# Spare TensorE products at two entries, and an attention pipeline whose transposes run one unit earlier

## The chip, the cores and the metric
The kernel runs on one core of a Trainium2 chip. The metric is device time in microseconds (us) of one execution, input loads and output stores included. Five engines work side by side, each through its own in-order list of instructions, and meet only at semaphores: TensorE (PE: matrix products and transposes), VectorE (DVE), ScalarE (ACT), GpSimd (POOL) and SyncE (SP: here only DMAs).

## The reference, cut to what matters
An activation of 4 x 1024 rows of 128 numbers passes through eight blocks, each `x = x + block(layernorm(x))`: a recurrent mixer with experts, a nine-path feed-forward, random-feature attention, the feed-forward again, segment attention, a soft decision tree, a linear recurrence, and the tree again. The change touches the entries of the third block and the whole of the fifth.

```python
# random features ("favor"): 16 heads of width 8, 32 features a head
phi(u) = exp(u @ proj - max(u @ proj)) * exp(-0.5 * sum(u * u)) + 1e-6
out = (phi(Q) @ (phi(K).T @ V)) / (phi(Q) @ sum(phi(K))) @ Wo.T + bo
# segments: 16 heads of width 8, segments of 64 rows
out = attn(q, k, v)                       # 64 x 64 in the own segment
for off in (-2, -1, 1, 2):                # every 4th row of four neighbours
    out += 0.25 * attn(q, k[seg + off, ::4], v[seg + off, ::4])   # if it exists
out = out @ Wo + bo
```

## The kernel before
Everything is float32 and stays on chip, with the 128 channels on the partitions and rows of x along the free axis: `k.X` holds the 4096 columns of x, `k.Y` the normalized ones, handled in eight chunks of 512. PSUM has eight banks of 512 columns: `k.bank[0..7]`, with `k.pair[i]` for two of them. A product with a 512-column float32 operand is recorded as two MATMULs.

`layernorm` (its lines L87 to L122) runs just ahead of either block: a product with `k.center` takes the mean out (L87, PE), ACT squares (L94), a product with `k.mean` gives the variance (L105, PE), ACT takes ln and exp (L114, L116), DVE writes `k.Y` (L122) and counts `ln_out`. Its last variance product lies well ahead of its last L122.

**Random features.** `favor` works on 32 half chunks: 16 of the keys, then 16 of the queries. PE's list starts with a wait for three copies of weights by DVE (`fw_copied`, L1564 to L1568), then a wait for the last of `ln_out`, then `project(0)` (L1581) and `norms(0)` (L1586, eight products of 16 columns). Then step s holds `scores(s)` (L1606, 16 products of 32 x 128), for the first half `gather` (L1622), `values` (L1593, even s), and the next `project` (even s) or `norms` (odd s). ACT copies and squares each projection (L1704, L1705), copies the norms (L1711), takes the exponentials (L1721) and copies the values (L1717). DVE's `statistics` takes maxima of the scores (L1775), adds the norms (L1782) and subtracts (L1786); in steps 1, 5, 9, ... a sum over `k.Y` (L1803) follows.

**Segments.** `segments` works on 64 units, n = 0 to 63, each eight heads of two segments; 16 units make a batch row, eight make one chunk of output. `first()` waits for weights and for the last `ln_out`, then issues six projections of batch row 0 (L1913) into banks 0 to 5. DVE moves the four for keys and values (L2144), ACT the two for queries in eight activations (L2005), POOL copies each fourth row next to its neighbours (L2077). `scores(0)` waits for these queries.

A unit goes through the engines in this order. PE `scores(n)` (L1937) waits until DVE is through with the scores of n-2. DVE `maxima(n)` (L2116, L2117), `shift(n)` (L2125, L2126; it writes one of four buffers `pr[n % 4]`, so it waits for the transposes of n-4). ACT `exp(n)` (L2037). POOL `halve(n)` (L2084), DVE `sums(n)` (L2133, L2135), ACT `weight(n)` (the reciprocal, L2041 and L2043), POOL `weigh(n)` (L2089, L2090). PE `turned(n)`: eight transposes (L1947) into `k.pair[2]`; ACT copies them (L2033). PE `weighed(n)`: 32 products (L1959) into bank 6. After eight units ACT's `heads(t)` (L2049) copies bank 6, PE's `output(t)` (L1977) multiplies by Wo, DVE's `add(t)` (L2140) adds to `k.X`. The first `weighed` of the next eight units waits for `heads(t)`, since it starts bank 6 anew.

What order there is, is written out by hand. Step n of PE's loop holds scores(n), turned(n-4), weighed(n-5), then, by tables of n, a projection of the next batch row (`PROJ`, L1919), the transposes of values (`values_at`, L1970) or an output. These three share bank 7 (`other`); `free()` makes each wait until the one before has been read: a projection by ACT (L2015, or L2005 in two halves for queries), values by ACT (L2026), an output by DVE's add. Step n of ACT's loop holds heads, turned(n-4), exp(n), weight(n-1), and the reads of bank 7. Step n of DVE's holds maxima(n), shift(n), the add, sums(n-1). In steps 65 and 66 PE also issues the first four L87 of the next norm (`after.center`).

Of the kernel before, what the change touches and what calls it, by code (L numbers as in the profile page):

```python
# [50 lines left out]
def plain(buf, c):  # L51

    return buf[:, c * CH:(c + 1) * CH]
# [161 lines left out]
def layernorm(k, block, norm, feed=None):  # L215

    k.ln_done, k.ln_logged = norm.n0 + NCH + PRIMED["ln_out"], norm.n0 + NCH

    @block.tensor
    def _(pe):  # L220
        for c in range(NCH + 2):
            if c >= 2:
                norm.variance(pe, c - 2)
            if c < NCH:
                norm.center(pe, c)
            if feed is not None:
                feed[0](pe, c)

    @block.scalar
    def _(act):  # L230
        activations(act, k, "natural_log_exp_and_others")
        norm.square(act, 0)
        norm.square(act, 1)
        for c in range(NCH):
            if c + 2 < NCH:
                norm.square(act, c + 2)
            norm.deviation(act, c)
            if feed is not None and len(feed) > 2:
                feed[2](act, c)

    @block.vector
    def _(dve):
        for c in range(NCH):
            norm.scale(dve, c)
            if feed is not None:
                feed[1](dve, c)


def ahead(after):
# [1253 lines left out]
def favor(nc, k, block, normalize, after):  # L1503
# [8 lines left out]
    N = 2 * HALF  # L1512
# [61 lines left out]
    def _(pe):  # L1574
# [91 lines left out]
            nc.tensor.matmul(other[:], wT[:, 3 * P:4 * P], o[c % 2], start=True, stop=True).then_inc(k.fv_out, 1)  # L1666

        pe.wait_ge(k.fw_copied, 3)
        pe.wait_ge(k.ln_out, normed)
        project(0)  # L1670
        norms(0)
# [186 lines left out]
def segments(nc, k, block, after):  # L1858
# [7 lines left out]
    N = B * NSEG  # L1866
# [20 lines left out]
    def own(v, b, c):  # L1887
        return v[b % 2][:, c * (NSEG // 2):(c + 1) * (NSEG // 2), 0:SEG]

    PROJ = {0: 0, 2: 1, 3: 2, 4: 3, 7: 4, 11: 5}  # L1890

    def project_at(n):
        return (n // 16 + 1) * 6 + PROJ[n % 16] if n < N - 16 and n % 16 in PROJ else None

    def values_at(n):
        return n // 4 if n < N and n % 4 == 1 else None

    def output_at(n):
        return (n - 14) // 8 if n >= 14 and n % 8 == 6 else None

    @block.tensor
    def _(pe):
# [5 lines left out]

        def first():
            pe.wait_ge(k.sw_in, 7 * 16)  # L1910
            pe.wait_ge(k.ln_out, normed)
            for i in range(6):
                nc.tensor.matmul(k.bank[i][:], k.sg_w[:, (1, 2, 0)[i // 2], :], k.Y[:, i % 2 * CH:(i % 2 + 1) * CH],  # L1913
                                 start=True, stop=True).then_inc(k.sg_proj, 1)

        def project(p):
            b, i = p // 6, p % 6
# [60 lines left out]
            last.append((k.sg_x, t + 1))  # L1978

        first()  # L1980
        for n in range(N + 7):
            if n < N:
                scores(n)
            if 0 <= n - 4 < N:
                turned(n - 4)
            if 0 <= n - 5 < N:
                weighed(n - 5)
            if project_at(n) is not None:
                project(project_at(n))
            if values_at(n) is not None:  # L1990
                values(values_at(n))
            if output_at(n) is not None:
                output(output_at(n))
            if n in (N + 1, N + 2):
                pe.wait_ge(k.sg_arg, n - 2)
                for c in range(2 * (n - N - 1), 2 * (n - N)):
                    after.center(pe, c)

    @block.scalar
    def _(act):  # L2000
# [51 lines left out]
        for c in range(2):  # L2052
            act.wait_ge(k.sg_proj, 5 + c)
            for part in range(2):
                queries(k.bank[4 + c], 0, c, part)
        for n in range(N + 7):
            if n >= 13 and n % 8 == 5:
                heads((n - 13) // 8)
            if 0 <= n - 4 < N:
                turned(n - 4)  # L2060
            if n < N:
                exp(n)
            if 0 <= n - 1 < N:
# [48 lines left out]
    def _(dve):  # L2112
# [37 lines left out]
        for n in range(N + 1):  # L2150
            if n < N:
                maxima(n)
                shift(n)
            if n >= 15 and n % 8 == 7:
                add((n - 15) // 8)
            if n >= 1:
                sums(n - 1)
        add(TURNS - 1)
# [393 lines left out]
```

## Time and profile before

| | us |
|---|---|
| median of 3 executions | 1256.6 (1256.03 to 1257.96) |
| the profiled execution: its time | 1258.29 |
| its span, first to last instruction | 1256.2 |
| PE busy in the span | 1139.7 (91%) |
| DVE busy | 930.1 (74%) |
| ACT busy | 815.3 (65%) |
| POOL busy | 230.7 (18%) |

All stretches below are us from the start of that span. PEclk is the clock granted to TensorE as a share of its upper level, 2.4 GHz; 0.50 is the lower, 1.2 GHz. The mean over the run is 0.95. PE's busy share includes work that took twice as long for the lower clock, so a busy PE says little until the clock of the stretch is read beside it.

### The profile page before, as it was taken

Reading aid. Unit: us, or ns where it says so; the run is one execution under the profiler, and the core shown is the slowest. Engines: PE = TensorE matmul, PEld = TensorE weight load, DVE = VectorE, ACT = ScalarE, POOL = GpSimd, SP = SyncE. Lnnn points to the kernel's source line nnn. Section 1 sums busy time; section 2 is a strip of 40 time slices with the busy share of each in tenths; the row PEclk is TensorE's granted clock in tenths of the full one; section 3 lists DMA queues with packets and bytes.
Section 4 is the critical chain, followed back from the end, with each engine's and each line's share of the span. In section 5 each row is a group of like instructions: output and inputs, shape, how many; then the busy total and the mean of one; then the engine's idle time right before and its main releaser. Section 6 shows DMA issues by size and latency. Waiting matters only on the chain.

```text
span 1256.2 us, 20246 instructions
## 1 busy us (share of the span) xinstructions
PE 1139.7 (91%) x7444; PEld 639.9 (51%) x7452; DVE 930.1 (74%) x1515; ACT 815.3 (65%) x1300; POOL 230.7 (18%) x330
## 2 busy tenths in 40 slices
PE   7899899999999999799998998798888888898787
PEld 3343344444444344377763453476666676463354
DVE  4967788777777767577775666697888896577766
ACT  6967555556556745645676547486777775868674
POOL 1000000000000011100000012486867675000000
PEclk9999999999999989989999999698899988999899
DMA  6000122122211000000000000000000000000002
GB/s 170 1 0 1 55 59 68 63 59 59 67 59 63 5 1 0 10 2 2 2 1 1 0 1 9 0 2 2 2 2 3 15 2 3 9 1 1 0 1 67
DMA packets 26362, 27.19 MB, mean 22 GB/s; under 512 B 4171, under 2 KB 17308, under 8 KB 26268
## 3 DMA queue, kind: packets, MB, share of 16 engines
q1 hardware_dynamic: 25936, 25.91, 6.9%
q8 instruction: 60, 0.98, 0.3%
q14 instruction: 34, 0.28, 0.1%
q10 hardware_dynamic: 332, 0.01, 0.0%
HBM read 23.30 MB, written 2.62 MB: 21 GB/s over the span
## 4 chain that ended last, share of the span: by engine, by line
PE 63%; DVE 17%; ACT 14%; issue 6%; DMA 0%; SPq 0%; DVEq 0%; ACTq 0%
PE psum L730 8%; PE psum L741 8%; PE psum L733 4%; PE psum L990 3%; PE psum L87 3%; PE psum L1937 3%; PE psum L962 3%; PE psum L1606 3%; PE psum L1947 2%; PE psum L1380 2%; DVE N L2126 2%; ACT ln_std L116 2%; ACT ln_std L114 2%; DVE arena L2117 2%; DVE arena L2116 2%
## 5 line engine op out<-in xcount | busy, mean ns | idle before, releaser
L769 ACT ACTIVATE arena<-psum 128x512 f32<-128x512 f32 x128 | 69.5, 595 | 114.5 <-PE psum L730 114.5
L730 PE MATMUL psum<-arena,weights 128*128 128x512 f32 x256 | 122.3, 601 | 1.7 <-DVE N L128 1.0
L741 PE MATMUL psum<-arena,weights 128*128 128x512 f32 x256 | 120.3, 593 | 0.0
L627 DVE SCALAR_TENSOR_TENSOR arena<-diff,vecs,N 128x512 f32<-128x512 f32 x128 | 95.2, 747 | 0.0
L2037 ACT ACTIVATE N<-N 128x1024 f32<-128x1024 f32 x64 | 67.8, 1059 | 41.7 <-DVE N L2126 41.4
L689 DVE SCALAR_TENSOR_TENSOR arena<-arena,psum 128x512 f32<-128x512 f32 x64 | 44.0, 688 | 62.5 <-PE psum L741 62.5
L1937 PE MATMUL psum<-arena 32*128 32x128 f32 x1024 | 84.6, 310 | 4.8 <-ACT arena L2005 4.8
L1937 PEld LDWEIGHTS psum<-arena 32*128 32x128 f32 x1024 | 71.1, 210 | 33.7 <-issue 18.7
L1947 PE MATMUL psum<-ident,N 128*128 128x128 f32 x512 | 77.2, 299 | 10.2 <-ACT arena L2033 9.9
L2033 ACT ACTIVATE arena<-psum 128x1024 f32<-128x1024 f32 x64 | 65.4, 1022 | 30.6 <-PE psum L1947 30.2
L730 PEld LDWEIGHTS psum<-arena,weights 128*128 128x128 f32 x256 | 48.6, 192 | 62.4 <-issue 58.0
L741 PEld LDWEIGHTS psum<-arena,weights 128*128 128x128 f32 x256 | 48.8, 190 | 61.1 <-issue 61.1
L105 PE MATMUL psum<-ln_sq,mean 128*128 128x512 f32 x144 | 73.2, 601 | 3.1 <-ACT arena L150 1.1
L87 PE MATMUL psum<-X,center 128*128 128x512 f32 x128 | 67.0, 618 | 6.5 <-DVE N L165 3.2
L1947 PEld LDWEIGHTS psum<-ident,N 128*128 128x128 f32 x512 | 61.2, 152 | 20.0 <-issue 15.1
L780 ACT ACTIVATE arena<-arena 128x1024 f32<-128x1024 f32 x64 | 68.3, 1067 | 0.0
L2090 POOL TENSOR_TENSOR N<-N,arena 128x512 f32<-128x512 f32 x64 | 67.8, 1060 | 0.0
L2089 POOL TENSOR_TENSOR N<-N,arena 128x512 f32<-128x512 f32 x64 | 66.8, 1044 | 2.1 <-ACT arena L2043 2.1
L2116 DVE TENSOR_REDUCE arena<-psum 128x8 f32<-128x512 f32 x64 | 43.9, 687 | 31.3 <-PE psum L1937 31.2
L733 PE MATMUL psum<-arena,weights 128*128 128x512 f32 x128 | 65.4, 593 | 0.0
L1775 DVE TENSOR_REDUCE arena<-psum 128x32 f32<-128x1024 f32 x32 | 39.2, 1224 | 32.8 <-PE psum L1606 32.8
L2084 POOL TENSOR_TENSOR mixed<-N 128x256 f32<-128x256 f32 x64 | 46.5, 727 | 74.4 <-ACT N L2037 74.3
(332 smaller groups left out, 2484.5 us busy)
## 6 DMA issues: line engine op xcount, KB each, us to landing
arena<-tw_rows SPq DMA_DIRECT2D x64, 256.0 KB, 3.1
out_dram<-arena SPq DMA_DIRECT2D x8, 256.0 KB, 3.6
arena<-in_L_attn_a_x_dram SPq DMA_DIRECT2D x3, 512.0 KB, 7.2
weights<-in_L_attn_a_eWk_dram SPq DMA_DIRECT2D x1, 1024.0 KB, 5.8
arena<-in_L_attn_a_x_dram SPq DMA_DIRECT2D x2, 256.0 KB, 4.1
weights<-in_L_attn_a_eWr_dram SPq DMA_DIRECT2D x1, 512.0 KB, 9.8
tw_rows<-arena SPq DMA_DIRECT2D x2, 128.0 KB, 2.7
tw_rows<-arena SPq DMA_DIRECT2D x1, 256.0 KB, 3.4
```

Of the source, the lines that this page charges most:

```text
L87: self.nc.tensor.matmul(k.bank[c % W][:], k.center[:], self.src(c), start=True, stop=True).then_inc(k.ln_centered, 1)
L105: self.nc.tensor.matmul(k.bank[W + c % self.vary][:], k.mean[:], k.ln_sq[:, c % W, :], start=True, stop=True).then_inc(k.ln_var, 1)
L627: op = nc.vector.scalar_tensor_tensor(mixed[:, n % 4, a, :], k.diff[:, q % 2, :], k.vec((f"cm_k{e}", f"cm_r{e}")[a]), before, ALU.mult, AL ...
L730: op = nc.tensor.matmul(k.bank[2 * (n % 2) + h][:], k.eWk[:, e, h * P:(h + 1) * P], mixed[:, n % 4, 0, :], start=True, stop=True)
L733: nc.tensor.matmul(k.bank[6][:], k.eWr[:, e, :], mixed[:, n % 4, 1, :], start=True, stop=True).then_inc(k.ex_r, 1)
L741: op = nc.tensor.matmul(k.bank[4 + n % 2][:], k.eWv[:, e, h, :], ks[:, (2 * (n % 2) + h) * CH:(2 * (n % 2) + h + 1) * CH], start=(h == 0), ...
L769: op = nc.scalar.activation(kr[:, h * CH:(h + 1) * CH], k.bank[2 * (n % 2) + h][:], ACT.Relu)
L780: nc.scalar.activation(ks[:, n % 2 * 2 * CH:(n % 2 + 1) * 2 * CH], kr, ACT.Square).then_inc(k.ex_sq, 1)
L1937: op = nc.tensor.matmul(scored[half][:, e * P:(e + 1) * P], k.sg_Q[b % 2][at, seg, 2 * j:2 * j + 2, :].rearrange("p h n -> p (h n)"), k.sg ...
L1947: op = nc.tensor.transpose(turned_to[:, e * P:(e + 1) * P], pr[n % 4][:, e * P:(e + 1) * P], k.ident[:])
L2037: nc.scalar.activation(pr[n % 4], pr[n % 4], ACT.Exp).then_inc(k.sg_exp, 1)
L2116: nc.vector.tensor_reduce(mx[n % 2][:, 0:8], mine, AX.X, ALU.max)
```

## The change
A helper issues products of `k.center` with the first chunk of x; nobody reads their result, no semaphore is counted. It is called with four products ahead of the `ln_out` wait in both blocks, and with five behind the six projections of segments. In the loops of segments, PE and ACT handle turned(n-3) in step n rather than turned(n-4), PE handles weighed(n-4), and the tables for bank 7, for heads and for the add move along. The steps after the last unit are one fewer.

```diff
+def keep_busy(nc, k, bank, products):
+    for _ in range(products):
+        nc.tensor.matmul(bank[:], k.center[:], plain(k.X, 0), start=True, stop=True)
 # favor, PE
         pe.wait_ge(k.fw_copied, 3)
+        keep_busy(nc, k, other, 4)
         pe.wait_ge(k.ln_out, normed)
 # segments, tables
-    PROJ = {0: 0, 2: 1, 3: 2, 4: 3, 7: 4, 11: 5}
+    PROJ = {0: 0, 1: 1, 3: 2, 4: 3, 7: 4, 11: 5}
-        return n // 4 if n < N and n % 4 == 1 else None              # values_at
+        return n // 4 if n < N and n % 4 == 2 else None
-        return (n - 14) // 8 if n >= 14 and n % 8 == 6 else None     # output_at
+        return (n - 13) // 8 if n >= 13 and n % 8 == 5 else None
 # segments, PE: first()
             pe.wait_ge(k.sw_in, 7 * 16)
+            keep_busy(nc, k, other, 4)
             pe.wait_ge(k.ln_out, normed)
             ...                                                      # six projections
+            keep_busy(nc, k, other, 5)
 # segments, PE: the loop
-        for n in range(N + 7):
+        for n in range(N + 6):
-            if 0 <= n - 4 < N: turned(n - 4)
-            if 0 <= n - 5 < N: weighed(n - 5)
+            if 0 <= n - 3 < N: turned(n - 3)
+            if 0 <= n - 4 < N: weighed(n - 4)
 # segments, ACT: the loop
-        for n in range(N + 7):
-            if n >= 13 and n % 8 == 5: heads((n - 13) // 8)
-            if 0 <= n - 4 < N: turned(n - 4)
+        for n in range(N + 6):
+            if n >= 12 and n % 8 == 4: heads((n - 12) // 8)
+            if 0 <= n - 3 < N: turned(n - 3)
 # segments, DVE: the loop
-            if n >= 15 and n % 8 == 7: add((n - 15) // 8)
+            if n >= 14 and n % 8 == 6: add((n - 14) // 8)
```

## Rows read from the trace of the kernel before

**Rows 1.** The page, chain that ended last: share of the span by engine.
```profile
PE 63%; DVE 17%; ACT 14%; issue 6%; DMA 0%; SPq 0%; DVEq 0%; ACTq 0%
```
**Rows 2.** Windows: stretch, length, busy us of each engine (instructions), clock, DMA.
```profile
527.50:546.00 18.50, 17.29 (x86) 13.63 (x86) 9.04 (x10) 5.10 (x9) 0.00 (x0) 0.54 0.00 1
795.50:818.40 22.90, 20.80 (x100) 13.23 (x100) 15.80 (x27) 9.25 (x19) 10.57 (x13) 0.50 0.00 0
```
**Rows 3.** Windows of 1 us, the same columns, where the clock falls.
```profile
528.00:529.00 1.00, 0.63 (x2) 0.00 (x0) 0.00 (x0) 0.33 (x1) 0.00 (x0) 0.95 0.00 0
781.00:782.00 1.00, 0.00 (x0) 0.00 (x0) 0.45 (x2) 0.56 (x1) 0.00 (x0) 0.74 0.00 0
```
**Rows 4.** Timeline, entry of favor: start, us, engine, line, tiles, count, [idle before <-releaser].
```profile
524.83 0.68 DVE L1568 COPY weights<-psum 128x512 f32<-128x512 f32 x1
526.70 0.69 DVE L122 TENSOR_TENSOR Y<-psum,ln_std 128x512 f32<-128x512 f32 x1 [0.55 <-ACT ln_std L116]
527.54 1.10 PE L1581 MATMUL psum<-Y,weights 128*128 128x512 f32 x2 [3.40 <-DVE Y L122]
529.81 1.89 PE L1586 MATMUL psum<-weights,arena 128*128 128x16 f32 x8 [1.18 <-ACT arena L1705]
533.75 1.23 DVE L1775 TENSOR_REDUCE arena<-psum 128x32 f32<-128x1024 f32 x1 [6.36 <-PE psum L1606]
543.29 1.22 DVE L1775 TENSOR_REDUCE arena<-psum 128x32 f32<-128x1024 f32 x1
```
**Rows 5.** Timeline, entry of segments.
```profile
782.43 8.31 PE L1913 MATMUL psum<-Y,weights 128*128 128x512 f32 x12 [3.40 <-DVE Y L122]
789.98 5.46 ACT L2005 ACTIVATE arena<-psum,weights 128x512 f32<-128x512 f32 x8 [8.42 <-PE psum L1913]
795.49 2.08 PE L1937 MATMUL psum<-arena 32*128 32x128 f32 x16 [4.75 <-ACT arena L2005]
797.61 0.69 DVE L2116 TENSOR_REDUCE arena<-psum 128x8 f32<-128x512 f32 x1 [3.42 <-PE psum L1937]
823.37 0.68 DVE L2116 TENSOR_REDUCE arena<-psum 128x8 f32<-128x512 f32 x1
```
**Rows 6.** Timeline, the same kinds of product at the upper clock.
```profile
521.29 1.02 PE L87 MATMUL psum<-X,center 128*128 128x512 f32 x2
548.61 1.06 PE L1586 MATMUL psum<-weights,arena 128*128 128x16 f32 x8
549.60 1.16 PE L1606 MATMUL psum<-weights,arena 32*128 32x128 f32 x16
```
**Rows 7.** Timeline, units of segments: a free pair of maxima, and two waits.
```profile
1039.87 0.68 DVE L2116 TENSOR_REDUCE arena<-psum 128x8 f32<-128x512 f32 x1
1043.30 0.68 DVE L2116 TENSOR_REDUCE arena<-psum 128x8 f32<-128x512 f32 x1
850.75 1.08 PE L1959 MATMUL psum<-arena,ln_sq 128*32 128x64 f32 x32 [2.10 <-ACT arena L2049]
854.93 0.69 DVE L2116 TENSOR_REDUCE arena<-psum 128x8 f32<-128x512 f32 x1 [3.43 <-PE psum L1937]
894.54 1.12 PE L1919 MATMUL psum<-Y,weights 128*128 128x512 f32 x2 [1.77 <-DVE X L2140]
896.80 0.69 DVE L2116 TENSOR_REDUCE arena<-psum 128x8 f32<-128x512 f32 x1 [1.40 <-PE psum L1937]
```
**Rows 8.** Waits, 820 to 1070: who for whom, us in total, times, longest.
```profile
DVE arena L2116 <- PE psum L1937: 23.6, 27, 3.4
```
**Rows 9.** The page, costliest groups: ACT's exp of a unit; busy us, mean ns.
```profile
L2037 ACT ACTIVATE N<-N 128x1024 f32<-128x1024 f32 x64 | 67.8, 1059 | 41.7 <-DVE N L2126 41.4
```
**Rows 10.** Timeline, the last unit of segments.
```profile
1061.46 1.06 POOL L2090 TENSOR_TENSOR N<-N,arena 128x512 f32<-128x512 f32 x1
1066.20 1.04 PE L1947 MATMUL psum<-ident,N 128*128 128x128 f32 x8
1068.35 0.65 PE L1959 MATMUL psum<-arena,ln_std 128*32 128x64 f32 x32 [0.53 <-ACT arena L2033]
```

More of the change, by code:

```diff
@@ L1980, in _ @@
         first()
-        for n in range(N + 7):
+        for n in range(N + 6):
             if n < N:
                 scores(n)
+            if 0 <= n - 3 < N:
+                turned(n - 3)
             if 0 <= n - 4 < N:
-                turned(n - 4)
-            if 0 <= n - 5 < N:
-                weighed(n - 5)
+                weighed(n - 4)
             if project_at(n) is not None:
@@ L2055, in _ @@
                 queries(k.bank[4 + c], 0, c, part)
-        for n in range(N + 7):
[L2057 to L2060, printed above, removed]
+        for n in range(N + 6):
+            if n >= 12 and n % 8 == 4:
+                heads((n - 12) // 8)
+            if 0 <= n - 3 < N:
+                turned(n - 3)
             if n < N:
@@ L2153, in _ @@
                 shift(n)
-            if n >= 15 and n % 8 == 7:
-                add((n - 15) // 8)
+            if n >= 14 and n % 8 == 6:
+                add((n - 14) // 8)
             if n >= 1:
```

## The prediction, made before the change was run
> **What bounds the kernel now.** I read the chain that ended last first: PE holds 63% of it and no other engine a fifth [rows 1], so PE's rate decides wherever the change works. Then the windows with the clock beside the busy time. In favor's first 18.5 us PE is busy 17.29 us at a clock of 0.54; in the first 22.9 us of segments' loop it is busy 20.80 at 0.50 [rows 2]. The one-microsecond windows show what came before each fall: PE stands idle for 3.40 us until the last L122, and the clock is at the lower level (1.2 GHz) from the end of window 528:529 in favor, and inside 781:782 in segments [rows 3, 4, 5]. There it falls twice: the six projections run mostly at half clock (8.31 us for twelve MATMULs), the clock returns, then PE waits 4.75 us for the queries and `scores(0)` takes 2.08 us, against 1.16 for 16 products of that shape at the upper level [rows 5, 6]. Behind the entries, in 820 to 1070, DVE is nearly the bound: free maxima stand 3.43 us apart [rows 7], and it still waits 23.6 us for scores [rows 8]. That sum is what a better order of the units could win at most; a worse order can add to it.
>
> **Favor, four spare products.** One costs two MATMULs, 0.43 us each at the upper clock: the pair's records take 1.02 with their overlap [rows 6], and I use 0.86. Four are 3.44 us. They start when DVE's copy ends, 524.83 + 0.68 = 525.5, and end at about 529.05. The projection starts at 527.54 now [rows 4], so it becomes 1.5 us late: they are longer than the gap they fill. What they may buy is the clock. From the projection to the norms is 2.27 us now (527.54 to 529.81) and stays so, since that projection already ran fast: norms at 531.3. At the upper clock the norms hold PE 1.0 rather than 1.9, `scores(0)` 1.16 rather than 2.08 [rows 4, 6]; DVE's first reduction comes at 533.5, now 533.75. Then values(0) and project(1), a microsecond each, stand ahead of scores(1): it ends at 536.6. Statistics take DVE 2.75 us, to 539.4, the sum over Y 1.2 more, so the third statistic starts at 540.6; now it starts at 543.29 [rows 4]. Gain 2.7 us. Further on the gain is not more, although PE could be earlier: the third projection's copies on ACT stand behind exp(2), which stands behind that third statistic, and norms(2) and scores(4) wait for them. Bounds: +1.5 if the clock falls all the same (every step as now, but late); on the other side PE's 17.29 us at 0.54 would be 9.3 at full clock, 8 less, with the 1.5 paid, -6.5. I take -2.7, from the walk along the rows.
>
> **Segments, the entry.** PE is free from 779.0 (782.43 less 3.40) and the weights are long in. Four products fill 779.0 to 782.45; the projections start at 782.43 now [rows 5], so these cost nothing. That cover is exact: with the clock at the lower level for part of them they would take up to 6.9 us and delay the projections by up to 3.4. At the upper clock six projections take 5.2 us. ACT starts on the queries after the fifth, 782.45 + 5 x 0.86 + 0.1 = 786.9, now 789.98: 3.1 us sooner. Its 5.46 us end at 792.4. The five spare ones behind the projections run 787.6 to 791.9, hidden behind ACT by 0.5 us; without ACT's span they would cost their full 4.3. DVE's moves and POOL's copies of keys start with the projections and stay ahead of the queries. So scores(0) comes 3.1 us sooner, at the upper clock.
>
> From maxima(0) to maxima(6) now pass 25.8 us (797.61 to 823.37) [rows 5]; at 3.43 a unit six take 20.6. So between 0 and 5.2 us more. The full 5.2 needs a clock that holds through new waits: project at n = 1 waits until ACT has read the one before, which lies behind exp(0), some 4.4 us after scores(0) ends (2.6 of DVE, four pieces like the 0.68 of [rows 7]; 1.06 for exp [rows 9]; some 0.7 for the copy), while PE has 2.2 us of work. I take 3: the clock probably falls once in the first few units, as it does now in the loop, and returns. The row of a fall behind a wait of this size is 850.75: 2.10 us idle, and the next 32 products took 1.08 us [rows 7], as long as at half clock.
>
> The Trainium skill speaks against this step ("TensorE: Matmul & The Clock Gate", "A second HAM failure mode: psum-queue depth-cycling"): short idles between groups of matmuls, often enough, make the clock swing between its levels though no one gap is long. This trace agrees at 850.75. By that rule the units gain nothing and only the 3.1 stay; it is rival A below.
>
> **A unit sooner, steady.** Turned(n-3) needs weigh(n-3), two steps of POOL closer. By the order on the engines, scores(n) is held by shift(n-2), and weigh(n-3) ends about 0.5 us after that shift (3.43-us units), when scores(n) still runs for 0.6 us: no wait, margin 0.6 us. DVE's shift no longer waits for transposes; that wait comes only at half clock, where PE is the bound anyway, so I count it nothing. What moves is bank 7 and bank 6. (a) The wait of weighed for heads stays (850.75, idle 2.10; DVE then waits 3.43) [rows 7], but values no longer stand between it and the next scores: 0.6 us less, four times, -2.4. (b) An output at n%8 = 5 is now followed by values at n%8 = 6, whose free() wants the add of DVE's own step n, behind shift(n): 2.6 + 0.74 us after the scores end, while PE has 1.6 us of work. PE idles 1.8 us, as now at 894.54 (1.77), where DVE lost 1.40 [rows 7]. There a projection followed; with values it is about 1.0. Now such a place occurs only before a projection at n = 7 of a batch row, twice; then seven times: 7 x 1.0 - 2 x 1.6 = +3.8. (c) Values leave n = 9, where they waited for ACT's half of the queries: -0.4 three times. (d) At n = 4 the heads wait now precedes a projection: +0.4 three times. Sum +1.4. Bounds: -8 where waits shrink enough that falls of the clock go (a third of the 23.6 of [rows 8]); +14 where each of seven new waits costs what 850.75 does, 3.4, less what is paid now. I take +1.
>
> **The end.** Now turned(63) runs at 1066.20, although POOL was through at 1062.5, because turned comes behind four products of the next norm in each of two steps; weighed(63) is at 1068.35 [rows 10]. A step sooner, turned(63) stands behind only the first batch of these, about 1063.6, and weighed(63) behind the second, about 1066.9: -1.5, and all of the next norm moves with it. Bounds 0 to -3.
>
> **Sum.** -2.7 - 3.1 - 3 + 1 - 1.5 = -9.3. The profiled execution took 1258.29, so 1249.0 for it; it stands 1.7 above the median of 1256.6. On the median: 1247.5.
>
> **Rivals.**
> A. The clock is lost again within a few units. Segments keeps 3.1 and the tail 1.5, favor about half of its gain or pays the 1.5, the loop +1 to +2: 1253 to 1255. For it: waits of 1 to 2.3 us in units 1 to 3, sparse products in favor. Against it: 894.54, where after 1.77 idle the scores still came in time with a loss of only 1.40.
> B. Slower: the add. Values at n%8 = 6 stop PE seven times for 1.8 us, two steps behind the heads wait of the same group; the clock falls at most of them and scores double. At 3.4 each, +24, less the 3 now paid, less 0.6 x 4, and less 10.3 won elsewhere: +8, 1264. It makes the kernel slower from about five of seven at that price (17 - 3 - 2.4 - 10.3 = +1). For it: [rows 7]. Against it: the heads wait alone already costs a fall at most places now, so many of the falls would only move.
> C. Better than forecast: the first units run at full clock (another 2.2), and falls in the loop go, since PE gets its work in evener steps: 5 more. 1240.
> D. The spare products don't hold the clock: 1.5 lost in favor, nothing won at either entry but the loop's shift: 1257.
>
> **Chances.** Forecast 0.45 (its own range 1244 to 1251), A 0.20, B 0.12, C 0.17, D 0.06. A difference under 0.2%, 2.5 us, can't be told from none. Faster: forecast, C and most of A, 0.77. Same: the rest of A and most of D, 0.11. Slower: B, 0.12. Range 1239 to 1257: it takes in C, the forecast and A, and leaves out B and the far ends.
>
> **What would show it.** Right: clock 1.00 in all 1-us windows from 524 to the first scores of favor and from 779 to scores(0) of segments; the first L1586 of favor at 531.3 with 1.06 us; favor's third L1775 at 540.6; the twelve MATMULs of L1913 in 5.2 to 5.3 us; L2005 starting 4.5 us after L1913; L1937 at once 1.16. In the loop a wait PE L1970 <- DVE L2140, seven times near 1.8, while DVE L2125 <- PE L1947 is gone. Wrong: L1913 still at 8 us (D); 0.50 in most windows of the first 15 us of the loop (A); DVE's waits for L1937 in the loop well over 23.6 us, each behind an L1970 (B); PE waiting for POOL L2090 ahead of L1947, for which I left 0.6 us.

## The result and the profile after

The changed kernel took 1242.4 us (median of 4 runs, 1237.8 to 1246.9) against 1257.3 (4 runs): ratio 0.988, interval [0.983, 0.993]. Measured once more in a later session it was 1240.95 (6 runs) against 1257.41 (11 runs), 0.9879 [0.9843, 0.9916]. The forecast was 1247.5 with a range of 1239 to 1257: the sign is right, but the gain is some 15 us and not 9, and most of it does not come from where the forecast put it. 1242.4 lies outside the forecast's own 1244 to 1251, between it and the 1240 of rival C.

Executions of one kernel differ here by up to 14 us. Some 5 us of it lie ahead of everything that was changed (the first 200 us run at a mean clock between 0.97 and 1.00 in kernels with the same code there), so the stages are compared by their own lengths and not by the total alone. A length of a stage comes from one profiled execution of each kernel; where several kernels share the code of a stage, all their lengths are given. The profiled execution took 1246.88 us with a span of 1244.7; the one of before 1258.29 and 1256.2.

The page of after: busy time and share of the span by engine, and the chain that ended last.
```profile
PE 1134.5 (91%) x7470; PEld 629.8 (51%) x7478; DVE 929.9 (75%) x1515; ACT 816.4 (66%) x1300; POOL 231.2 (19%) x330
PE 61%; DVE 18%; ACT 12%; issue 7%; POOL 1%; DMA 0%; SPq 0%; DVEq 0%; ACTq 0%
```
PE holds 61% of the chain where it held 63% [rows 1], DVE one point more.

The timeline of after, entry of favor (start, us, engine, line, tiles, count, [idle before <-releaser]). L252 is the spare product, L1587 the projection, L1592 the norms, L1612 the scores.
```profile
526.28 3.70 PE L252 MATMUL psum<-X,center 128*128 128x512 f32 x8 [1.44 <-DVE weights L1574]
529.82 1.02 PE L1587 MATMUL psum<-Y,weights 128*128 128x512 f32 x2
532.02 1.06 PE L1592 MATMUL psum<-weights,arena 128*128 128x16 f32 x8 [1.17 <-ACT arena L1712]
533.01 2.01 PE L1612 MATMUL psum<-weights,arena 32*128 32x128 f32 x16
549.52 1.32 PE L1592 MATMUL psum<-weights,arena 128*128 128x16 f32 x8 [2.94 <-ACT arena L1712]
550.77 2.08 PE L1612 MATMUL psum<-weights,arena 32*128 32x128 f32 x16
```
Windows of after over the same stretch (the clock is the third figure from the end):
```profile
526.00:533.00 7.00, 5.54 (x18) 2.79 (x18) 1.56 (x3) 2.44 (x5) 0.00 (x0) 1.00 0.00 0
533.00:538.00 5.00, 5.00 (x27) 3.92 (x26) 2.64 (x3) 0.41 (x2) 0.00 (x0) 0.51 0.01 3
550.00:556.00 6.00, 6.00 (x60) 5.25 (x60) 2.64 (x3) 1.53 (x3) 0.00 (x0) 0.52 0.01 3
```
The gap before the projection is filled and the norms run in 1.06 us, as forecast. Then the clock goes to the lower level all the same: at 533 behind an idle of 1.17, at 550 behind one of 2.94, and a third time at 570.7. The second is norms(2) waiting for ACT, a wait that the prediction named as a bound on the gain and did not take for a risk to the clock. Counted from the last L122 (the end of the norm ahead of favor), the third statistic comes 0.2 us later than before, the sixth 3.3 and the tenth 5.0; 1.7 come back at the twentieth, where the kernel before has a fall (604 to 607) and this one has none. To favor's last statistic pass 138.9 us, before 135.5: favor lost 3.3 us.

The timeline of after, entry of segments (L1921 first projections, L2014 queries, L1946 scores, L1928 later projections, L2125 maxima).
```profile
786.49 5.42 PE L1921 MATMUL psum<-Y,weights 128*128 128x512 f32 x12
791.75 4.46 PE L252 MATMUL psum<-X,center 128*128 128x512 f32 x10
796.66 1.16 PE L1946 MATMUL psum<-arena 32*128 32x128 f32 x16 [0.47 <-ACT arena L2014]
797.87 0.69 DVE L2125 TENSOR_REDUCE arena<-psum 128x8 f32<-128x512 f32 x1 [2.51 <-PE psum L1946]
802.20 1.55 PE L1928 MATMUL psum<-Y,weights 128*128 128x512 f32 x2 [2.23 <-ACT arena L2024]
803.68 2.08 PE L1946 MATMUL psum<-arena 32*128 32x128 f32 x16
821.40 0.68 DVE L2125 TENSOR_REDUCE arena<-psum 128x8 f32<-128x512 f32 x1
1040.96 0.69 DVE L2125 TENSOR_REDUCE arena<-psum 128x8 f32<-128x512 f32 x1 [0.93 <-PE psum L1946]
```
Against [rows 5]: the twelve MATMULs take 5.42 us and not 8.31, the scores 1.16 and not 2.08, and from the first projection to maxima(0) pass 11.38 us where 15.18 did. At unit 1 PE waits 2.23 us for the keys, and the clock is down for ten microseconds.

Windows of after, segments' loop.
```profile
775.00:802.00 27.00, 24.43 (x82) 10.60 (x81) 15.49 (x22) 17.01 (x28) 4.77 (x9) 1.00 0.00 1
803.00:813.00 10.00, 9.72 (x49) 6.36 (x48) 7.82 (x14) 6.48 (x14) 6.56 (x8) 0.50 0.01 2
820.00:860.00 40.00, 34.40 (x620) 26.97 (x619) 37.00 (x65) 33.74 (x64) 31.15 (x37) 1.00 0.01 2
900.00:940.00 40.00, 35.73 (x595) 26.46 (x592) 36.39 (x64) 33.49 (x65) 30.92 (x36) 1.00 0.01 2
980.00:1020.00 40.00, 36.39 (x622) 30.09 (x623) 36.51 (x64) 27.98 (x53) 27.55 (x31) 0.87 0.04 12
```
Windows of before, the same stretches.
```profile
820.00:860.00 40.00, 35.20 (x564) 27.22 (x565) 34.23 (x60) 32.40 (x62) 30.30 (x36) 0.87 0.01 2
900.00:940.00 40.00, 35.11 (x559) 27.65 (x557) 33.62 (x60) 30.33 (x60) 27.10 (x31) 0.87 0.01 2
980.00:1020.00 40.00, 34.50 (x571) 28.29 (x570) 35.46 (x62) 29.82 (x58) 27.90 (x31) 0.87 0.04 12
```
In the first 40 us PE does 56 more instructions in less busy time. From maxima(6) to maxima(63) pass 219.56 us, before 230.27: 10.7 us, nearly the whole result, from the part that the forecast gave +1.

Waits of after, 815 to 1045 (who for whom: us in total, times, longest us).
```profile
DVE arena L2125 <- PE psum L1946: 16.2, 29, 1.0
PE psum L1979 <- DVE X L2149: 12.4, 7, 1.8
PE psum L1956 <- POOL N L2099: 8.2, 16, 1.2
PE psum L1968 <- ACT arena L2058: 4.9, 7, 1.1
```
The same of before, 818 to 1055.
```profile
PE psum L1959 <- ACT arena L2049: 9.9, 7, 2.4
PE psum L1947 <- ACT arena L2033: 7.3, 9, 1.7
DVE N L2125 <- PE psum L1947: 5.0, 8, 0.7
```
The wait of the weighing for the heads, 1.95 to 2.39 us at four places and under 1 us at three, is now at most 1.1; seven waits of 1.8 for the add have come. DVE's own waits for scores went from 23.6 [rows 8] to 16.2, and none is over 1.0 us where one was 3.4. DVE's waits for the transposes (the last line), 5.0 us in eight, are gone; all eight stood at the lower clock.

How such a wait and the clock go together in the kernel before: the heads wait of unit 29 (919.69), then the scores, which slow down on their way, and the clock in the windows.
```profile
919.69 0.65 PE L1959 MATMUL psum<-arena,ln_sq 128*32 128x64 f32 x32 [2.39 <-ACT arena L2049]
920.86 1.59 PE L1937 MATMUL psum<-arena 32*128 32x128 f32 x16
920.00:921.00 1.00, 1.00 (x31) 0.74 (x22) 0.59 (x2) 1.00 (x2) 0.14 (x1) 1.00 0.00 0
921.00:922.00 1.00, 1.00 (x14) 1.00 (x16) 0.00 (x0) 0.97 (x5) 0.52 (x1) 0.71 0.00 0
```

The two spans by stage: to the last L122 +0.7; favor +3.3; between favor's last statistic and segments' first projection 0.0; to maxima(0) -3.8; to maxima(6) -2.2; to maxima(63) -10.7; to the last output +0.35; behind it +0.8. Together -11.5, the difference of the spans.

### The profile page after: what moved, and what is told of

Its sections match the earlier page's. It is cut to its first block, busy times and chain, and to the rows that moved or that the text cites. A ratio compares the mean times of both kernels' runs of the same rounds, so it can differ in the third digit from the quotient of the medians.

```text
span 1244.7 us, 20296 instructions
## 1 busy us (share of the span) xinstructions
PE 1134.5 (91%) x7470; PEld 629.8 (51%) x7478; DVE 929.9 (75%) x1515; ACT 816.4 (66%) x1300; POOL 231.2 (19%) x330
## 4 chain that ended last, share of the span: by engine, by line
PE 61%; DVE 18%; ACT 12%; issue 7%; POOL 1%; DMA 0%; SPq 0%; DVEq 0%; ACTq 0%
PE psum L736 8%; PE psum L747 8%; PE psum L739 4%; PE psum L87 4%; PE psum L996 4%; PE psum L968 3%; PE psum L1946 3%; PE psum L1612 2%; PE psum L1386 2%; DVE arena L2126 2%; DVE N L2135 2%; PE psum L105 2%; ACT ln_std L114 1%; ACT ln_std L116 1%; ACT N L2046 1%
## 5 line engine op out<-in xcount | busy, mean ns | idle before, releaser
L1956 PE MATMUL psum<-ident,N 128*128 128x128 f32 x512 | 72.8, 287 | 12.0 <-POOL N L2099 11.0
L1946 PEld LDWEIGHTS psum<-arena 32*128 32x128 f32 x1024 | 64.9, 193 | 26.5 <-issue 13.8
L1946 PE MATMUL psum<-arena 32*128 32x128 f32 x1024 | 77.4, 291 | 0.5 <-ACT arena L2014 0.5
L87 PE MATMUL psum<-X,center 128*128 128x512 f32 x128 | 69.8, 642 | 6.5 <-DVE N L165 3.2
L1956 PEld LDWEIGHTS psum<-ident,N 128*128 128x128 f32 x512 | 57.3, 145 | 21.9 <-POOL N L2099 16.1
L2098 POOL TENSOR_TENSOR N<-N,arena 128x512 f32<-128x512 f32 x64 | 66.9, 1045 | 2.1 <-ACT arena L2052 2.1
L2125 DVE TENSOR_REDUCE arena<-psum 128x8 f32<-128x512 f32 x64 | 43.9, 686 | 22.2 <-PE psum L1946 22.0
L94 ACT ACTIVATE ln_sq<-psum 128x512 f32<-128x512 f32 x72 | 41.9, 591 | 28.0 <-PE psum L87 28.0
```

The costliest lines, as they stand in the source:

```text
L87: self.nc.tensor.matmul(k.bank[c % W][:], k.center[:], self.src(c), start=True, stop=True).then_inc(k.ln_centered, 1)
L1946: op = nc.tensor.matmul(scored[half][:, e * P:(e + 1) * P], k.sg_Q[b % 2][at, seg, 2 * j:2 * j + 2, :].rearrange("p h n -> p (h n)"), k.sg ...
L1956: op = nc.tensor.transpose(turned_to[:, e * P:(e + 1) * P], pr[n % 4][:, e * P:(e + 1) * P], k.ident[:])
```

## Experiments

The first four take the change apart, on one chip beside the kernel before (1256.37, 27 runs). A ratio and its interval are not the quotient of the medians; the two differ by up to 0.2%.

**Favor's four spare products alone.** The kernel before, plus
```
         pe.wait_ge(k.fw_copied, 3)
+        keep_busy(nc, k, other, 4)
         pe.wait_ge(k.ln_out, normed)
```


> The kernel before with the four spare products ahead of the last ln_out wait of favor alone. My theory of the result: they hold the clock through the projection, it falls all the same about 3 us later in some executions, so the gain of 2.7 us that I forecast is there in some and a loss of up to 3 in others: ratio 0.997 to 1.002, and the spread of the executions wider than that of before. Rival 1, the prediction as it stood: -2.7 us, ratio 0.998, clock 1.00 up to the first scores. Rival 2, the spare products only cost their excess over the gap: +1.5, ratio 1.001.

1258.47 us (12 runs), ratio 1.0026 [1.0002, 1.005]: they cost. From the last L122 to the last statistic 138.8 us, as in the changed kernel; the clock fell at 531, 542, 549 and 569. The forecast's -2.7 is out. The excess of 1.5 alone lies inside the interval, but not the stage's 3.3; and the executions do not spread wider than those of before (8.9 us against 12.1), so the expected mixture of gains and losses is not seen.

**The nine at segments' entry alone.** The same line with 4 in `first()` of segments and one with 5 behind its six projections.

> The kernel before with the four and five spare products at the entry of segments alone, the loop as before. Theory 1 (the loop's own order is what took away the falls of the clock): first reduction of scores 3.8 us sooner after the first projection, the six units after it 2 us sooner, and then the same falls of the clock in the loop as before, so -5 to -6 us in all, ratio 0.9955. Rival (the clock in the loop hangs on the entry, the new order adds little): falls go here too, -12 to -16 us, ratio 0.989.

1250.80 (12 runs), 0.9975 to before [0.9952, 0.9998], -5.6 us by the medians (by the interval -6.0 to -0.3). First projection to maxima(0) 11.38 us (-3.8), to maxima(6) 23.64 (-2.1); maxima(6) to (63) 231.7, as before, with the clock at 0.84 to 0.96 in the 40-us windows. So the entry gives what it gives at the entry, and nothing of the loop's gain is its work: the rival is out.

**The loop alone, no spare products.**
```
-    PROJ = {0: 0, 2: 1, 3: 2, 4: 3, 7: 4, 11: 5}
+    PROJ = {0: 0, 1: 1, 3: 2, 4: 3, 7: 4, 11: 5}
-        return n // 4 if n < N and n % 4 == 1 else None
+        return n // 4 if n < N and n % 4 == 2 else None
-                turned(n - 4)
+                turned(n - 3)
```
(with weighed, heads, output and add one step sooner, as in the change)

> The changed loop of segments without any spare product. Theory 1 (the loop's order takes the falls of the clock away by itself): units 6 to 63 take 219 to 221 us as in the changed kernel, entry as before, -9 to -12 us in all, ratio 0.992. Rival (as I forecast for the loop: +1, end -1.5): ratio 1.000, with windows at half clock behind the heads waits as before.

1244.68 (10 runs), 0.9917 [0.9888, 0.9946], -11.7 us by the medians. The profiled execution, 1236.04, is one of its two fastest. Its windows:
```profile
820.00:860.00 40.00, 34.90 (x594) 26.52 (x594) 37.02 (x65) 33.83 (x61) 31.36 (x36) 1.00 0.01 2
900.00:940.00 40.00, 35.49 (x612) 26.38 (x612) 36.57 (x64) 31.58 (x58) 30.72 (x36) 1.00 0.01 2
980.00:1020.00 40.00, 33.35 (x632) 27.27 (x633) 38.65 (x69) 30.48 (x58) 30.36 (x34) 1.00 0.02 5
```
The clock never falls in them, and maxima(6) to (63) takes 217.18 us, 13.1 less than before. Since nothing fills a gap here, the order alone keeps the clock; the rival, the forecast's +1, is out. From maxima(6) to maxima(63) the old loop has seven falls in each of its three profiles (before, favor alone, entry alone), 41 to 44 us at the lower clock. The new one has none here (one comes just behind maxima(63)), 2 in after with 10 us, and 16 in nine profiles together (after, this one, and those of the experiments below but for the two that alter the loop).

Where these falls stand, for every wait of PE of 1 us or more: how many waits there are, and how many had a fall within 4.4 us of the start of the idle.

| PE waits for | us | waits | falls |
|---|---|---|---|
| old order, three profiles: the heads | 1.9 to 2.4 | 12 | 12 |
| the add | 1.8 | 6 | 3 |
| ACT's copy, ahead of transposes | 1.7 | 6 | 3 |
| ACT's queries, ahead of values | 1.2 | 3 | 3 |
| new order, nine profiles: the add | 1.8 | 63 | 17 |
| the heads | 1.1 to 1.3 | 27 | 0 |
| POOL, ahead of transposes | 1.0 to 1.2 | 28 | 1 |

(Two of the 17 come just behind maxima(63).) So four of the old loop's seven falls go with the heads, and the other three with waits that the new order moved as well.

**The change without favor's four.**

> The changed kernel without the four spare products of favor; segments as changed. Sum of theory 1: -16 us against before, ratio 0.987 to 0.988, and a narrower spread than the changed kernel's 1237.8 to 1246.9, since favor's clock is what makes two groups of times. Rival: the two groups come from segments and stay here.

1239.14 (6 runs), 0.988 [0.9846, 0.9914], -17.2 us by the medians: the sum of the two parts (-5.6 - 11.7 = -17.3). By the ratios it is 0.9975 + 0.9917 - 1 = 0.989. The parts add within their intervals, and favor's products are the only one with the wrong sign. Its executions spread over 6.9 us, the changed kernel's over 9.1, and two of its six stand 3 us under the rest; that favor makes two groups of times is not shown.

**Two in favor instead of four** (a second chip, before 1256.88, 8 runs; the next three too).

> The changed kernel with two spare products at favor's entry in place of four: 1.7 us of work for a gap of 1.9 us. Theory (the four cost their 1.5 us excess, and favor's clock falls later for idles inside its first units, whatever the entry does): the projection 0.1 us behind the last L122 again, the clock falls once or twice in the first 30 us, statistics 0 to 31 take 128 to 131 us; 1 to 3 us less than the changed kernel. Rival (the entry decides favor's clock, and two do as well as four): statistics 0 to 31 in 126 us or less and no window under 1.00.

1239.85 (4 runs), 0.9874 [0.9846, 0.9901]. The timeline of its entry:
```profile
525.55 1.98 PE L252 MATMUL psum<-X,center 128*128 128x512 f32 x4 [1.44 <-DVE weights L1574]
527.43 1.12 PE L1587 MATMUL psum<-Y,weights 128*128 128x512 f32 x2
529.73 1.07 PE L1592 MATMUL psum<-weights,arena 128*128 128x16 f32 x8 [1.18 <-ACT arena L1712]
530.72 1.16 PE L1612 MATMUL psum<-weights,arena 32*128 32x128 f32 x16
```
Two end just as the norm does; the projection is not late and the first scores take 1.16. The clock falls later and for shorter (532 to 536 and 539 to 543, before 529 to 546). That is the theory; the rival is out, since maxima of statistics 0 to 31 take 127.3 us. From the last L122 to the last statistic, in all profiles:

| in favor | us |
|---|---|
| none (before and six kernels) | 135.5, 135.5, 135.5, 135.5, 135.1, 133.7, 138.3 |
| two (this and two later ones) | 132.5, 132.5, 132.5 |
| four (after, alone, after again) | 138.9, 138.8, 140.8 |

Against the usual 135.5 two win 3.0 us, four lose 3.3 to 5.3. The table is of the stage; by the total this kernel and the one with none (1239.14) are not told apart. One kernel with none, at 138.3, is nearly as slow as those with four: there a second fall came at 545, where the usual profile has none until 599.

**The later gaps of favor filled.** One more spare product ahead of norms(0), three ahead of norms(2), with four at the entry.
```
         def norms(c):
+            if c in (0, 2):
+                keep_busy(nc, k, k.bank[6], 1 if c == 0 else 3)
```


> The changed kernel, and one spare product into bank 6 ahead of norms(0), three ahead of norms(2), where PE stood idle 1.2 us and 2.9 us. Theory (the clock of favor falls behind these idles, of which I had named the second only as a bound on the gain): clock 1.00 from the entry to at least 560, the fourth to sixth statistics 3.1 to 4.1 us apart in place of 6.0 and 6.0, -4 to -6 us against the changed kernel, so about 0.984 of before. Rival (sparse products, 16 or 32 columns or rows, lose the clock, not the idles): the windows behind scores(0) are at 0.50 as they were, and the spare products cost up to 3 us more.

1239.17 (4 runs), 0.9883 [0.9845, 0.992]; 136.0 us by the table's measure. The clock held through the first statistics (the second came 3.0 us behind the first, 5.4 in after), then PE waited 2.32 us for norms(1) and it fell at 534; the three products ahead of norms(2) made that late. It was the only fall in favor, 7 us, and yet the stage was no shorter than with none, so the clock is not its whole price; how much the spare products themselves cost there was not taken apart. The theory wanted the clock up to 560 and 4 to 6 us; it fails, and so does the rival, since the clock held through the sparse products of scores(0). Here the filled gap hands the fall on to the next one.

**A longer single wait in the loop.** The kernel without favor's products, with ACT's heads behind its `weight(n - 1)` instead of first in the step.

> The changed segments without favor's spare products, and ACT's heads moved from the start of its step to behind weight(n-1). PE's wait for it at n%8 = 4 grows from 1.1 and 0.3 us to about 3.5 us, seven times. Theory (length of one idle is what brings the clock down in the loop): it falls behind most of these, units behind them take 5 us and more, and the loop from unit 6 to 63 takes 235 us or more, against 219. Rival (only the wait counts, the clock holds as the loop is otherwise even): each costs 1.5 to 2.5 us of DVE, 219 + 7 x 2 = 233 at most, all windows of the loop at 1.00.

1283.16 (4 runs), 1.0214 [1.0175, 1.0253]. Its waits, 815 to 1060:
```profile
DVE arena L2124 <- PE psum L1945: 55.4, 35, 5.5
PE psum L1967 <- ACT arena L2057: 22.7, 6, 3.9
PE psum L1978 <- DVE X L2148: 10.6, 6, 1.8
```
PE's waits for the heads, at most 1.1 without this edit, are 3.75 to 3.93 (six here, a seventh at 1062), and the 40-us windows read 0.79 to 0.91 instead of 1.00. Against the same kernel with the heads first, maxima(6) to (60) takes 42.3 us longer (to (63) 48.2): about 26 in the six units that wait, the other 16 in the units behind them, at the lower clock. A fall follows each of the seven heads waits, and each of the seven waits of 1.76 for the add two units on, where without the long wait 17 of 63 have one. The theory holds, the rival is out. These waits are longer than those of the old loop, so the run shows that a long wait there brings the clock down, not from what length on.

**Without the wait for the add.** Every second group's values at n%8 = 7, and one projection at 8 instead of 7.

> The changed segments without favor's spare products; the transposes of values of every second group of four go from n%8 = 6 to n%8 = 7, a step behind DVE's add, and the projection of n = 7 goes to 8. Theory (the 0.93 us that DVE loses at each of seven places is the wait for the add, as forecast at 1.0): no PE L1970-kind wait for the add is left, DVE's units at 15, 23, ... lose 0.74 for the add alone, loop -5 to -6.5 us. Rival (the wait comes back at the next user of bank 7, which waits for ACT's copy of the values): -1 to -3 us, with waits of projections at n = 0 and 8 grown instead.

1242.93 (5 runs), 0.9899 [0.9866, 0.9933]: no gain. The wait is gone, but the weighing now waits for the values' copy (10.5 us in all, eight times), which no expectation had; maxima(6) to (63) 221.9 us, against 218.9 for the same kernel without the move, where both theory and rival had a gain. Three falls here and two there make part of the difference. The add's 7 x 0.93 cannot be had by this move.

**The wait in unit 1 and the tail** (the second chip again, before 1257.41, 11 runs; also for the next two).
```
+            if n in (N + 1, N + 2):
+                (the two center products, moved from here ...)
             if 0 <= n - 3 < N:
                 turned(n - 3)
             if 0 <= n - 4 < N:
                 weighed(n - 4)
-                (... behind turned and weighed)
+            if n == 1:
+                keep_busy(nc, k, k.bank[4], 2)
```


> The changed kernel without favor's four spare products, with the two waits that were still followed by a fall of the clock closed: two spare products into bank 4 ahead of unit 1's projection, and in the last two steps the two center products each ahead of the transposes instead of behind them. In the kernel without favor's spare products the projection of unit 1 waited 2.23 us for ACT's keys and the clock was down for some nine units' worth of microseconds behind it; maxima(0) to maxima(6) took 23.54 us, and in the tail of the changed kernel transposes(62) waited 2.74 us for POOL, the four center products behind them took 3.15 us. Theory (the length of one idle brings the clock down, and the clock is what was lost): no row under 1.00 between the entry and unit 12, maxima(0) to (6) about 21.5 us (6 x 3.44 = 20.6 and some waiting for the fill), the transposes' wait in the tail under 1.2 us, maxima(63) to the last output about 14.5 us against 16.5; together -3.5 us beside the kernel without favor's products, a ratio near 0.985 to the kernel before. Rival (these stretches are bound by the chain ACT, POOL and DVE form for the first units and for the last, and PE's clock in them is no part of it): the clock holds but maxima(0) to (6) stays within 0.7 us of 23.5 and the tail within 0.5 of 16.5.

1238.69 (6 runs), 0.9865 [0.9836, 0.9894]. Its timeline at units 1 to 3:
```profile
794.72 1.98 PE L252 MATMUL psum<-X,center 128*128 128x512 f32 x4
797.02 1.13 PE L1927 MATMUL psum<-Y,weights 128*128 128x512 f32 x2 [0.32 <-ACT arena L2025]
799.93 0.66 PE L1978 MATMUL psum<-ident,arena 128*128 128x128 f32 x4 [0.70 <-ACT arena L2025]
804.46 2.07 PE L1927 MATMUL psum<-Y,weights 128*128 128x512 f32 x2 [1.59 <-ACT ln_sq L2036]
806.46 2.08 PE L1945 MATMUL psum<-arena 32*128 32x128 f32 x16
```
The fall moved from unit 1 to unit 3, so maxima(0) to (6) took 24.4 us, no less than the 23.5 without the fill: the theory fails as it was put, and the rival too, since the clock did not hold. In the tail, maxima(63) to the last output took 13.76 us, against 16.52 and 14.93 in the two profiles of the changed kernel: there the theory holds. (The expectation has the clock down for nine units' worth behind unit 1; it was 10.2 us, three units.)

**The changed kernel again.**

> The changed kernel once more, on the chip of its variants, so that favor's four, two and no spare products stand on one chip. Theory (four are 1.5 us too long for the gap and only move the fall to norms(2)): between 2 and 4 us above the kernel without them, ratio near 0.989 to 0.990 to the kernel before. Rival (four or none make no difference, the two medians seen before are from different chips): within 0.7 us of it.

1240.95 (6 runs), 2.3 above the kernel before this one, which also has two more edits; the intervals overlap, so by the total favor's four are not told apart from none. By the stage they are (140.8 us). This profile shows the new loop without one fall: maxima(6) to (63) 217.13 us, and the tail 14.93, 1.24 less than before. But the first units are worse: the fall at unit 1, behind the same wait of 2.23 us, lasts from 797.9 to 815.0, and maxima(0) to (6) takes 26.64 us, more than the 25.75 of before.
```profile
798.00:815.00 17.00, 16.73 (x107) 11.23 (x108) 11.33 (x21) 9.76 (x21) 10.90 (x14) 0.50 0.00 1
```
Over the five profiles of the new order with the entry's spare products and no other edit in the segments, maxima(0) to (6) takes 23.5 three times, 26.6 here and 22.0 with two in favor, with the clock down for 10, 17 and 7 us.

**Two in favor, with both edits.**

> The changed kernel with two spare products in favor instead of four, and with both waits closed as in the kernel of the two spare products in unit 1. Two products ended with the statistics' wait and cost the first projection nothing: favor's statistics 0 to 31 took 127.28 us with them, 128.46 with none, 131.22 with four. Theory (each fall of the clock costs by itself, so the gains add): the fastest of all, about 1.2 us under the kernel with no favor products and both waits closed, some 1234 us, ratio 0.983. Rival (what favor gains there is lost again before the segments begin, since its later waits are long enough to bring the clock down whatever was done at the entry): within 0.5 us of the kernel with no favor products.

1237.91 (5 runs), 0.9843 [0.9811, 0.9875]. Favor again 132.5 us; maxima(0) to (6) 24.3, tail 13.6. Only 0.8 us under its neighbour (1238.69) by the median, too little to tell theory from rival.

**Two more in unit 3** (the first chip, before 1257.23, 9 runs).
```
-            if n == 1:
-                keep_busy(nc, k, k.bank[4], 2)
+            if n in (1, 3):
+                keep_busy(nc, k, k.bank[4] if n == 1 else k.bank[6], 2)
```


> The kernel with two spare products in favor, two in unit 1 and the tail's center products first, and two more spare products (into bank 6, which the first weighing writes only later) ahead of unit 3's projection. With unit 1's wait filled the fall of the clock only moved to unit 3, where the projection waited 1.59 us for ACT's values (after waits of 0.32 and 0.70); units 4 and 5 took 2.43 and 1.46 us over 3.44 and maxima(0) to (6) 24.26 us, against 23.53 to 23.54 in two profiles with nothing filled. Theory (what unit 3 to 5 lose is the clock at half: projection and scores 2.08 us instead of 1.12 and 1.16): the rows of units 3 to 5 stand at 1.00 and maxima(0) to (6) takes 21 to 22.5 us. Rival 1 (the fall moves on once more, to the next wait in units 4 to 8): the fall comes later and maxima(0) to (12) gains under 1 us. Rival 2 (units 4 and 5 wait for the chain ACT, POOL and DVE form, not for PE's clock): clock at 1.00 there and maxima(0) to (6) still above 23.5.

1233.35 (5 runs, 1230.7 to 1234.6), 0.9811 [0.9784, 0.9838]: the fastest by the median, 24 us under before, though the interval overlaps with that of the kernel before this one. Its timeline there:
```profile
798.52 1.88 PE L252 MATMUL psum<-X,center 128*128 128x512 f32 x4
800.27 1.12 PE L1928 MATMUL psum<-Y,weights 128*128 128x512 f32 x2
801.33 1.16 PE L1946 MATMUL psum<-arena 32*128 32x128 f32 x16
```
All one-microsecond windows from 796 to 816 read 1.00, units 4 and 5 lose 0.56 and 0.31 us where they lost 2.43 and 1.46, and maxima(0) to (6) takes 21.24 us, the least of all profiles. The theory holds for these units and rival 2 is out. Rival 1 is half right: the fall did move on, to 823.9 in unit 9, behind 1.24 us of waiting for POOL ahead of the transposes, but maxima(0) to (12) takes 43.97 us where it took 46.00, a gain of 2.0 and not under 1. The unfilled kernels took 45.3 as a rule and 43.7 in the one whose fall was short, so one profile does not give the size of the gain.

## Why the prediction was right and wrong

**Segments' entry: right, with luck in its second part.** Forecast -3.1 for the queries; the queries start 4.66 us behind the first projection (before 7.55, forecast 4.5), and with the scores' own 0.9 us it is -3.8 to maxima(0). The loop's first six units: -3 forecast, -2.2 measured, with the one fall that was expected, at the wait that was named (project at n = 1); in the second profile of the change, where that fall lasted 17 us, they were +0.9. Rival D is out: the spare products hold the clock. The sign set for rival A did appear, 0.50 in nine of the loop's first fifteen microseconds, and did not mean what it was to mean: the loop behind it kept the clock.

**The loop, "a unit sooner, steady": the step that failed.** Its sum was +1.4 with +1 taken and -8 as its bound; measured -10.7, and -13.1 in each of the two profiles whose loop has no fall (the second profile of the change, and the loop alone). The single waits were sized well: the add stops PE seven times for 1.76 to 1.77 us (forecast 1.8) and costs DVE 0.93 each (forecast 1.0). What was left out is the clock. The 57 intervals of before exceed 3.44 us by 34.2 us, and 22.0 of these lie in eleven units (13 to 14: 3.50, 15: 2.68, 27, 28, 30, 31, 40, 46, 47, 62, 63) that stand in or right behind a fall. The other 46 exceed it by 12.3, which is 15 us for 57 (an estimate); the new loop without a fall exceeds it by 21.1. So by its waits alone the new order is some 6 us slower, the sign that the forecast gave it, and the falls cost the old one some 19. Maxima(6) to (12), where neither has a fall, agree with that: 21.18 us before, 21.74 after.

Two terms of the forecast hid that. Part (a), the heads, was priced as 0.6 us less of waiting, four times; but each of the twelve heads waits of 1.9 to 2.4 us in the three old profiles had a fall with it, and none of the 27 of 1.1 to 1.3 in the new ones. And DVE's wait for the transposes was put at nothing, since it comes only at the lower clock; it does, and it was 5.0 us, which went with the falls. The experiment that lengthens the heads wait shows that this wait can bring the clock down. For the three falls of seven that stood behind other waits, which of the moves took them away is open; that the order as a whole did is shown by the loop alone. Rival C had the mechanism ("falls in the loop go"), at 5 us and a chance of 0.17. Rival B's fear, that an idle of 1.8 would do the same, is a matter of frequency: it did behind 12 of the first 54 of these waits and 17 of all 63, and behind all seven where a longer wait stood two units ahead.

The Trainium skill ("TensorE: Matmul & The Clock Gate", "A second HAM failure mode: psum-queue depth-cycling") says that frequent short idles make the clock swing. Here it held in favor and, with the gap of unit 1 filled, in unit 3, where a fall followed idles of 0.70 and 1.59 us; in the loop, with a wait of 1.8 each eight units, 46 of 63 such waits had no fall behind them. So the direction of the rule is seen and its reach is not general.

**Favor: wrong sign, -2.7 forecast, +3.3 measured.** The 1.5 us by which four products overrun the gap was in the sum; what failed is the walk behind it, which supposed the clock held through the first scores and statistics. It fell at 533 (the first scores took 2.01 us), and the third statistic came at 544.2 (forecast 540.6, or 541.3 with the 0.7 us by which the norm itself was later). The lower bound of +1.5, "every step as now, but late", was too mild as well: PE waited 2.94 us for norms(2), where before it did not wait at all, and there were two falls in the first 30 us where before had one. Most of the 3.3 us comes behind that second fall, and the third. Two products, which the same rows would have given (3.4 us of gap less 1.4 until the copy is done is room for two), win 3.0 in this stage.

**The tail: -1.5 forecast, +0.35 in the first profile, -1.24 in the second.** In the first the transposes of unit 62 waited 2.74 us for POOL, the clock fell and the four center products behind took 3.15 us instead of 1.98; in the second a fall had come at 1036.8, behind the last wait for the add, PE was later, that wait was 1.74 and no second fall followed. So the term, -1.5, was nearly met in one profile and missed in the other, and it had no place for the wait for POOL at unit 62.

**The wait for POOL ahead of the transposes: margin wrong, cost mostly nothing.** 0.6 us of margin was forecast; PE waited 16 times, up to 1.2 us, and DVE's next maxima were not late for it. It was not free everywhere: in the last experiment a fall came behind one of 1.24 us, and maxima(6) to (12) took 22.73 us where the other profiles of this order have 21.75.

The total came near by luck, because errors of opposite sign met. In the profiled executions (forecast -9.3, measured -11.5) the loop gave 11.7 more than its term, favor 6.0 and the tail 1.8 less, the entry was 0.1 off, and the stages that nobody touched cost 1.5.

## What to carry to other kernels

An idle stretch of the matrix engine is priced in two parts: the wait itself, and whether the clock is lower behind it; in this loop the second part was the larger, and it was to be read from the slow units of the trace (22 of 34 us in eleven of 57). Spare products must end with the gap: in favor two where there was room for two won 3 us of the stage, four lost 3. And a filled gap handed the fall to a later idle three times here (to norms(1), to unit 3, to unit 9); look at the whole row of waits before filling the first.

## What the runs showed of the hardware

The length of an idle does not decide alone whether the clock falls. In the loop, waits of 1.9 to 2.4 us had a fall with them in 12 of 12 cases, and so had those of 2.2 to 2.9 named above in favor, unit 1 and the tail; waits of 1.76 us had one in 17 of 63 cases of the new order, but in 7 of 7 where a wait of 3.8 stood two units ahead; one of 1.23 had it in all three old profiles at the same place, while of 28 of 1.0 to 1.24 in the new order one had; and 1.59 had it where it stood 4 us behind one of 0.70. That is how two profiles of one kernel have different loops (219.56 and 217.13 us), and part of why its executions spread. What also surprised: the way back takes very different times. Behind the same wait of 2.23 us at unit 1, in kernels with the same code there, the clock was back after 7, 10 or 17 us; behind the falls of the loop after 3 to 10; at the entry of favor without spare products it took 17 (524 to 541 in the kernel without favor's four), although PE's records show it busy 16.6 of these 17 us. Why, no run here shows. Nor is it settled what makes one of the 63 equal waits bring the clock down and the next one not.
